# Gated attention stages of a hybrid transformer layer put back to back, with norms and routing inside them and expert work moved later

## What is computed

```
x = x + gated_attention(layernorm(x))   # "a": groups of 32 tokens, INNER 256
x = x + moe_ffn(layernorm(x))           # "f": 8 experts, top 2 of softmax(x @ Wr), capacity 160 a row
x = x + attention_16_heads(layernorm(x))# "c": softmax over 1024 x 1024 scores, 16 heads of 64
x = x + moe_ffn(layernorm(x))           # the same weights as the first FFN
```

## Time and profile before

| what | us |
|---|---|
| median of 3 runs | 1641.32 |
| the profiled execution | 1643.49 |
| its span, first to last instruction | 1641.5 |
| PE, DVE, ACT, POOL busy in the span | 1511.9, 1049.9, 881.9, 271.4 |
| start of the pairs (first L747) | 238.82 |

### The profile page before, as it was taken

One profiled execution on the slowest core, in us unless ns is written; L12 is line 12 of the kernel. 1 busy time (PEld: TensorE's weight loads), 2 busy tenths in 40 slices (PEclk: granted clock), 3 DMA queues, 4 the chain that ended last, 5 costly groups with the idle time before them and its releaser, 6 DMA issues.

```text
span 1641.5 us, 24653 instructions
## 1 busy us (share of the span) xinstructions
PE 1511.9 (92%) x9488; PEld 739.6 (45%) x9488; DVE 1049.9 (64%) x2187; ACT 881.9 (54%) x1697; POOL 271.4 (17%) x295
## 2 busy tenths in 40 slices
PE   6688989999999999999999999999999999999531
PEld 6587973333444333334443333344433334444231
DVE  6755837787555677865556888655568865556601
ACT  3334645555655555556555555665555555655221
POOL 3217443021000120200002103000021030000433
PEclk9799999999999999999999999999999999999766
DMA  8402121001000110110001101100021011000111
GB/s 236 153 22 68 40 71 39 14 25 35 14 14 14 39 30 14 33 33 7 14 14 42 45 21 30 30 14 14 3 56 36 14 32 27 14 14 1 44 43 55
DMA packets 45957, 60.05 MB, mean 37 GB/s; under 512 B 6915, under 2 KB 33952, under 8 KB 45712
## 3 DMA queue, kind: packets, MB, share of 16 engines
q1 hardware_dynamic: 36208, 39.57, 8.7%
q0 software_dynamic: 9632, 18.91, 4.0%
HBM read 23.83 MB, written 20.97 MB: 27 GB/s over the span
## 4 chain that ended last, share of the span: by engine, by line
PE 86%; DVE 3%; issue 3%; POOL 3%; DMA 2%; ACT 1%; POOLq 0%; DVEq 0%; ACTq 0%; SPq 0%
PE bank L801 30%; PE bank L811 27%; PE bank L747 8%; PE bank L762 4%; PE bank L752 4%; POOL xslots L499 3%; PE bank L910 2%; PE bank L905 2%; PE bank L322 2%; PE bank L311 1%; DMA slots_sb<-xslots 1%; PE bank L618 1%; PE bank L900 1%; POOL yg L510 1%; ACT hT L411 1%
## 5 line engine op out<-in xcount | busy, mean ns | idle before, releaser
L828 ACT ACTIVATE prob<-bank,nmx 128x1024 f32<-128x1024 f32 x512 | 565.9, 1110 | 513.6 <-DVE nmx L819 513.6
L819 DVE TENSOR_REDUCE nmx<-bank 128x1 f32<-128x1024 f32 x512 | 603.1, 1220 | 212.0 <-PE bank L801 211.7
L801 PE MATMUL bank<-q,k 64*128 64x512 f32 x1024 | 509.9, 616 | 2.5 <-ACT prob L828 1.7
L801 PE MATMUL bank<-q,ks 64*128 64x512 f32 x1024 | 506.5, 616 | 0.0
L811 PE MATMUL bank<-prob,vsc 128*64 128x512 f32 x2048 | 485.3, 595 | 0.0
L801 PEld LDWEIGHTS bank<-q,k 64*128 64x128 f32 x1024 | 170.6, 186 | 209.7 <-issue 127.7
L801 PEld LDWEIGHTS bank<-q,ks 64*128 64x128 f32 x1024 | 170.6, 186 | 122.3 <-issue 117.6
L811 PEld LDWEIGHTS bank<-prob,vsc 128*64 128x64 f32 x2048 | 139.8, 137 | 186.7 <-issue 184.2
L1214 POOL DMA_INDIRECT yg<-yslots,row_ring x80 | 80.5, 1006 | 811.2 <-PE bank L801 791.9
L835 DVE RECIPROCAL zinv<-zsum 128x2 f32<-128x2 f32 x256 | 42.4, 165 | 184.2 <-ACT prob L828 183.6
L747 PE MATMUL bank<-xT,wqkv_sb 128*64 128x512 f32 x512 | 137.4, 617 | 0.0
(11 more groups left out here) (209 smaller groups left out, 1395.4 us busy)
## 6 DMA issues: line engine op xcount, KB each, us to landing
ks<-k SPq DMA_DIRECT2D x64, 256.0 KB, 3.1
slots_sb<-xslots SPq DMA_DIRECT2D x8, 640.0 KB, 4.6
yslots<-slots_sb SPq DMA_DIRECT2D x8, 640.0 KB, 3.7
xslots<-xhat_r POOLq DMA_DIRECT2D x5, 512.0 KB, 7.1
yslots<-xhat_r POOLq DMA_DIRECT2D x5, 512.0 KB, 13.0
w_sb<-in_w SPq DMA_DIRECT2D x1, 2048.0 KB, 8.3
wqkv_sb<-in_wqkv SPq DMA_DIRECT2D x1, 2048.0 KB, 18.7
xslots<-xhat_r,row_s POOLq DMA_INDIRECT x128, 2.2
```

Of the source, the lines that this page charges most:

```text
L801: ins = nc.tensor.matmul(bank[:, SC[h][n], :], kk[r, cols(j)], qst[pi % 2][r, cols(n, HALF)], start=True, stop=True)
L819: nc.vector.tensor_reduce(nmx[:, 2 * s + h:2 * s + h + 1], bank[:, SC[h][0]:SC[h][0] + 2, :], mybir.AxisListType.XY, ALU.max, negate=True) ...
L828: nc.scalar.activation(prob[s][h][:].rearrange("p (n c) -> p n c", c=HALF), bank[:, SC[h][0]:SC[h][0] + 2, :], ACT.Exp, bias=nmx[:, 2 * s ...
```

## The change

Rows 0, 1 and 2 of the attention now run without experts between them; experts 0 follow stage 2, then stage 3, experts 1, experts 2 and the pairs. The pieces between the stages move into them:

- The norm of the next row, and from stage 1 on the norm of the row before for its FFN, are split: DVE makes mean, variance and rstd and a shift (`norm_stats_vector`), ACT writes the normed row (`xhat_scalar`, eight activations in place of DVE's L212), PE transposes it inside the stage, before L618. ACT waits, before it overwrites `xhat_r` in stages 2 and 3, for the scatter of the row before last (`f_sc`).
- Logits and the choice of experts of row r - 1 come at the end of stage r. The counts and slot numbers of row 0 come in the middle of stage 2 (PE waits for `f_idx` ahead of its last two token blocks of v); those of rows 1 and 2 in experts 0 and 1.
- The bias that DVE added (L219) is now added by POOL (`a_bias_gpsimd`), ahead of the scatters. PE waits for the residual of the stage before (`a_res`) ahead of v, and for all four v's ahead of the linear scores (v's banks are swapped).
- Answers go to a buffer of their own (`ans_sb`), so that a row's slots can be loaded while the answers of the one before are still stored. `xslots` and `yslots` are four tensors each; only `xslots` is zeroed, with 2.6 MB where 5.2 MB were written.
- Only row 0 is gathered in the head. Rows 1 and 2 are gathered and combined beside steps 0 to 33 of the pairs (`first_gathers`, `COMBINE_0`).
- In the tail DVE's statistics come ahead of a wait, and two small copies go (`wtok`, `row_g`).

The core of the diff:

```diff
+        def norm_stats_vector(v, step, c0, b, done):
+
+            stats_vector(v, step, c0, b, range(T))
+            aggr_vector(v, step, c0)
+            newton_vector(v, step, c0, NEWTON, True)
+            c = slice(c0, c0 + T)
+            nc.vector.scalar_tensor_tensor(out=shift[:, c], in0=meanvar[:, c, 0], scalar=-1.0, in1=rstd[:, c],
+                                           op0=ALU.mult, op1=ALU.mult).then_inc(done, 1)
+
+        def xhat_scalar(a, c0, b, xh, done):
+
+            for t in range(T):
+                c = c0 + t
+                ins = nc.scalar.activation(xh[:, t, :], row_of(b, t), ACT.Identity, bias=shift[:, c:c + 1], scale=rstd[:, c:c + 1])
+                if t % 4 == 3:
+                    ins.then_inc(done, 1)
+
...
-        V_BANK = [0, 1, 6, 7]
+        V_BANK = [6, 7, 0, 1]
...
+        def a_tensor(pe, r):
+            if r == B - 1:
+                pe.wait_ge(f_idx, 2)
...
+            if r > 0:
+                pe.wait_ge(a_res, 2 * r)
             for t in range(T):
                 if t == 4:
                     pe.wait_ge(a_xs, 2 * r + 2)
+                    if r == 2:
+                        positions(pe, 0)
+                if t == 6 and r == 2:
+                    pe.wait_ge(f_idx, 1)
                 x_hi, x_lo, o = xT_hi[:, cols(t)], xT_lo[:, cols(t)], bank[:, V_BANK[t // 2], cols(t % 2, INNER)]
                 nc.tensor.matmul(o, x_hi, wa_hi[:, WVA:], start=True, stop=False)
                 nc.tensor.matmul(o, x_hi, wa_lo[:, WVA:], start=False, stop=False)
...
-            pe.wait_ge(a_vbias, 4 * r + 2)
+            pe.wait_ge(a_vbias, 4 * r + 4)
...
-            if with_experts:
-                pe.wait_ge(a_state, 7 * (r + 1))
+                if e == 0 and r > 0:
+                    f_norm_tensor(pe, r - 1, FTR)
+            if r < B - 1:
                 pe.wait_ge(a_gated, 4 * r + 2)
-                slots_tensor(pe, r - 1, THIRD_A)
+                a_norm_tensor(pe, r + 1, ATR)
+            if r > 0:
+                logits_tensor(pe, r - 1, LG)
...
+            if r > 0:
+                a.wait_ge(lf_stat, r)
+                if r > 1:
+                    a.wait_ge(f_sc, 256 * (r - 1))
+                xhat_scalar(a, 0, r - 1, xhat_r, lf_xhat)
...
+            if r < B - 1:
+                a.wait_ge(la_stat, r + 1)
+                a.wait_ge(la_tr, 2 * r + 2)
+                xhat_scalar(a, T, r + 1, xhat, la_xhat)
+            if r > 0:
+                f_norm_scalar(a, r - 1, FTR)
+            if r < B - 1:
+                a_norm_scalar(a, r + 1, ATR)
+            if r > 0:
+                probs_scalar(a, r - 1)
+
+        def a_vector(v, step, r):
+            b = r
+            if r > 0:
+                norm_stats_vector(v, step, 0, r - 1, lf_stat)
...
+            if r == 2:
+                route_place_vector(v, step, 0, 0)
...
+            if r < B - 1:
+                if r == 0:
+                    v.wait_ge(load_x, 16)
+                norm_stats_vector(v, step, T, r + 1, la_stat)
...
+            if r > 0:
+                route_choose_vector(v, step, r - 1, LG)
+            if r < B - 1:
+                a_low_vector(v, r + 1)
+            v.wait_ge(a_bias, r + 1)
...
+        def a_bias_gpsimd(p, r):
+
+            xb = xres[:, r * T:(r + 1) * T, :]
+            hold(p, la_xhat, 2 * r + 2)
+            nc.gpsimd.tensor_tensor(xb, xb, bout_sb[:].unsqueeze(1).to_broadcast([P, T, P]), ALU.add).then_inc(a_bias, 1)
...
+        COMBINE = {2: (0, 0, 4), 3: (0, 4, 8), 5: (1, 0, 4), 6: (1, 4, 8)}
+        COMBINE_0 = {5: (1, 0, 0, 4), 6: (1, 0, 4, 8), 8: (1, 1, 0, 4), 9: (1, 1, 4, 8),
+                     30: (2, 0, 0, 4), 31: (2, 0, 4, 8), 32: (2, 1, 0, 4), 33: (2, 1, 4, 8)}
...
+        def first_gathers(p):
+
+            for m, g0 in ((1, 0), (2, 10)):
+                hold(p, f_comb, 2 * T * m)
+                hold(p, f_st, 16 * (m + 1))
+                for k in range(2):
+                    for t in range(T):
+                        if t % 2 == 0:
+                            paced(p, g0 + (k * T + t) // 2)
+                        gather_tile(p, m, k, t, f_ga)
...
+            for b in range(B):
+                nc.gpsimd.dma_start(xslots[b][0:S, :].rearrange("(t p) c -> p t c", p=P), xhat_r[:]).then_inc(zeroed, 16)
+                nc.gpsimd.dma_start(xslots[b][S:, :].rearrange("(t p) c -> p t c", p=P), xhat_r[:, 0:ST - T, :]).then_inc(zeroed, 16)
             p.wait_ge(zeroed, ZEROED)
-            for b in range(B):
-                if b > 1:
-                    gather(p, step, b - 1, b - 2)
-                if b < B - 1:
-                    scatter(p, b + 1)
+            for r in range(3):
+                a_bias_gpsimd(p, r)
+            scatter(p, 0, 0)
+            a_bias_gpsimd(p, 3)
+            scatter(p, 1, 1)
+            gather(p, 0, 0)
+            scatter(p, 2, 2)
...
+            for r in range(3):
+                a_scalar(a, r)
+                if r == 1:
+                    a.wait_ge(zeroed, ZEROED)
+            a.wait_ge(load_f, 112)
+            slots_scalar(a, 0)
+            experts_scalar(a, 0, lambda e: None)
+            a_scalar(a, 3)
+            slots_scalar(a, 1)
+            experts_scalar(a, 1, lambda e: None)
+            slots_scalar(a, 2)
+            experts_scalar(a, 2, lambda e: first_norm_scalar(a) if e == E else None)
...
+            a_low_vector(v, 0)
+            for r in range(3):
+                a_vector(v, step, r)
+            route_place_vector(v, step, 1, 1)
+            a_vector(v, step, 3)
+            route_place_vector(v, step, 2, 2)
+            combine_vector(v, step, 0, 0)
...
+            a_tensor(pe, 0)
+            pe.wait_ge(load_f, 112)
+            a_tensor(pe, 1)
+            a_tensor(pe, 2)
+            pe.wait_ge(la_xT, 8)
+            pe.wait_ge(f_sub, 2)
+            slots_tensor(pe, 0)
+            experts_tensor(pe, 0, lambda e: positions(pe, 1) if e == 1 else None, (a_res, 6))
+            a_tensor(pe, 3)
+            pe.wait_ge(f_sub, 3)
+            slots_tensor(pe, 1)
+            experts_tensor(pe, 1, lambda e: positions(pe, 2) if e == 1 else None, (a_res, 8))
+            slots_tensor(pe, 2)
+            experts_tensor(pe, 2, lambda e: first_norm_tensor(pe, 2) if e == E else None, (f_ys, 6))
```

More of the change, by code:

```diff
@@ L215, in bias_vector @@
-        def bias_vector(v, step, n, b, bias):
-            xb = xres[:, bass.ds(b * T, T), :]
-            v.wait_ge(ln_xhat, (n + 1) * T)
-            step.done(nc.vector.tensor_tensor(xb, xb, bias[:].unsqueeze(1).to_broadcast([P, T, P]), ALU.add))
-        def xT_scalar(a, n):
-            for h in range(2):
-                c = slice(h * HALF, (h + 1) * HALF)
-                a.wait_ge(ln_tr, 2 * n + h + 1)
-                nc.scalar.activation(xT[:, c], bank[:, LN_MAIN + h, :], ACT.Copy).then_inc(ln_xT, 1)
-                a.wait_ge(ln_xT, 2 * n + h + 1)
-                nc.scalar.activation(xT_hi[:, c], xT[:, c], ACT.Copy).then_inc(ln_hi, 1)
@@ L243, in ln_scalar, with row_of, stats_vector @@
-        def ln_scalar(a, n, dst, bk):
-            for h in range(2):
-                a.wait_ge(ln_tr, 2 * n + h + 1)
-                nc.scalar.activation(dst[:, h * HALF:(h + 1) * HALF], bank[:, bk + h, :], ACT.Copy).then_inc(ln_xT, 1)
         def cols(i, n=P):
             return slice(i * n, (i + 1) * n)
+        def row_of(b, t):
+            return xres[:, b * T + t, :]
+        def stats_vector(v, step, c0, b, tiles):
+            for t in tiles:
+                step.done(nc.vector.bn_stats(stats[:, c0 + t, :], row_of(b, t)))
@@ new lines, in xhat_scalar, with transposes @@
+        def xhat_scalar(a, c0, b, xh, done):
+            for t in range(T):
+                c = c0 + t
+                ins = nc.scalar.activation(xh[:, t, :], row_of(b, t), ACT.Identity, bias=shift[:, c:c + 1], scale=rstd[:, c:c + 1])
+                if t % 4 == 3:
+                    ins.then_inc(done, 1)
+        def transposes(pe, xh, half, bk):
+            for t in range(4):
+                ins = nc.tensor.transpose(bank[:, bk, cols(t)], xh[:, 4 * half + t, :], ident[:])
+            return ins
@@ new lines, in a_norm_tensor, with a_norm_scalar @@
+        def a_norm_tensor(pe, r, bk):
+            for h in range(2):
+                pe.wait_ge(la_xhat, 2 * r + h + 1)
+                transposes(pe, xhat, h, bk + h).then_inc(la_tr, 1)
+        def a_norm_scalar(a, r, bk):
+            for h in range(2):
+                c = cols(h, HALF)
+                a.wait_ge(la_tr, 2 * r + h + 1)
+                nc.scalar.activation(xT[:, c], bank[:, bk + h, :], ACT.Copy).then_inc(la_xT, 1)
+                a.wait_ge(la_xT, 2 * r + h + 1)
+                nc.scalar.activation(xT_hi[:, c], xT[:, c], ACT.Copy).then_inc(la_hi, 1)
@@ new lines, in a_low_vector, with f_norm_tensor, f_norm_scalar @@
+        def a_low_vector(v, r):
+            for h in range(2):
+                c = cols(h, HALF)
+                v.wait_ge(la_hi, 2 * r + h + 1)
```

(21 more changed lines are left out.)

473 lines of the change are left out of this document (172 added, 301 removed).

## The result

The changed kernel takes 1669.77 us (median of 4, 1668.21 to 1670.82), the kernel before, beside it, 1641.99 (4 runs, 1640.40 to 1643.72): ratio 1.0168, 95% interval 1.0151 to 1.0186. The profiled execution has a span of 1669.0 against 1641.5, so 27.5 of it can be read in the traces.

A forecast was written before the change was run, and what follows sets the result against it. The head was taken to go at the pace of a loop of route, scatter, load and experts; pairs 17.9 later plus 0.5 within them made 18.4, hence 1661.9 profiled and 1659.7 us forecast, 8 in 10 within 1650 to 1669.

The forecast's parts named there:

- row 1 starts at 45.3: End of stage 0: row 1's first projection on PE starts at 45.3 us, 20 us gained so far.
- full-clock unit: A stage's PE work at full clock: 11.5, 9.9 and 3.6 us, 25.0 in all, with the out-projection taking 3.84.
- Stage 1: Stage 1: 33.2 us of PE work with additions, out-projection done at 78.5, then PE stands 2.5 until 81.5.
- the wait in stage 2: ACT waits for row 0's scatter before overwriting `xhat_r`; PE stands 21.5 us, from 101.3 to 122.8.
- The wait before the last slots: In experts 2, PE stands 13.7 us for row 2's scatter and load; slots reach it at 232.9.
- the faster one: Rival: ACT finds row 0's scatter through and stage 2 runs on; pairs at 234.4, time 1637.4; chance 0.07.
- Late weights: Rival: zeroing isn't shortened, w2 lands at 51.8, PE stands 6.5 us at 45.3; time 1666; chance 0.06.
- Low clock for longer: Rival: after stands of 21 and 14 us, stage 2 stays at half clock through its sums, +5: 1665; chance 0.10.
- POOL's bias: Rival: through the shared port the bias blocks DVE's low part, 0 to 10 us; 1665 at 5 each; chance 0.06.
- cancelled the loss: Rival: gains elsewhere, DVE's stretches 10% shorter and the last wait halved, cancel the loss: 1641; chance 0.02.
- Pairs: Pairs: four more quarters of a combination on DVE add 0.5 us, ends 0 and 4.5.
- table-load drain: Exp loads ending stages 1 and 2: skill's 1380 ns drain would add 1.4 at the first; left out.

The follow-up runs named there:

- fifteenth run: Changed kernel with PE kept busy at the ends of stages 0 to 2, row 0 handed over by tiles, POOL's bias behind the low part: 1667.49 us, ratio 1.0154.
- fourteenth run: Changed kernel with row 0's normed rows handed to PE tile by tile, not by halves: 1669.79 us, ratio 1.0163.
- seventh run: Changed kernel with all four stages ahead of the experts and a second buffer for row 1's normed FFN rows: 1638.07 us, ratio 0.9970.
- thirteenth: Changed kernel with PE multiplying constants while it would stand at the ends of stages 0 to 2: 1668.88 us, ratio 1.0154.
- tenth: Changed kernel with ACT's scatter wait and `xhat_r` activations moved behind v's silus, keys and squares: 1694.9 us beside 1702.8 for the kernel before.
- seventeenth: Changed kernel with ACT's scatter wait and `xhat_r` activations moved behind v's silus, keys and squares: 1650.48 us, ratio 1.0051.
- third run: Changed kernel with PE multiplying constants while it would stand at the ends of stages 0 to 2: 1709.1 us beside 1712.3 for the kernel before.
- fourth run: Changed kernel with POOL's bias waiting for both low parts of the next row: 1710.1 us beside 1712.3 for the kernel before.
- first run: Changed kernel with a second buffer for row 1's normed FFN rows: 1695.2 us beside 1712.3 for the kernel before.

## Why the prediction came out low

The order of events was right, and so were direction and cause. The steps, in us on each clock: as forecast, in the changed kernel, and with the three sizes mended (fifteenth run):

```
                          forecast  changed  mended
row 1 starts                 45.3    49.89    46.02
row 2 starts                 81.5    86.83    81.37
slot numbers of row 0        93.9    98.27    94.44
key-value products 2        122.8   127.18   123.34
stage 2 done                143.5   149.62   145.93
experts 0 done              166.1   172.12   168.42
stage 3 done                197.1   205.29   199.46
slot numbers of row 2       205.3   213.47   207.64
slots of row 2 on PE        232.9   240.94   235.22
pairs start                 256.7   265.45   259.56
```

**The step that failed** is "row 1 starts at 45.3": the length of stage 0, 4.6 of the 8.8 us by which the pairs are later than forecast. Three terms were mis-sized, two by going on with full clock and the old hand-over.

(1) The key-value products start at 29.54, in the forecast's trace at 27.30. Row 0 is handed over by halves, an edit that I had not costed: the first projection starts at 15.15 instead of 14.40, which is 0.75. The rest is when the products quicken: they come 0.43 apart until 21.3 instead of 17.1. That moment varies in the same code: the kernel before, run again (sixth), starts these products at 28.82. Over all profiled executions they start at 28.2 to 29.5 by halves (fifteen, mean 28.9) and at 27.3 to 28.8 by tiles (five, mean 27.9). So the hand-over is worth about 1 us, and what the fourteenth run shows, 2.0, is in part luck.

(2) PE stands 2.6 us for the gates, which I had; the out-projection behind it then runs at a granted 0.50 and takes 5.76, which I had at 3.84. Kept busy, it took 3.74. The trace of before had the warning. I took its full-clock unit from stage 0, but behind PE's waits for slots the same 32 products took longer in stages 1 to 3:

```profile
95.88 5.37 PE L618 MATMUL bank<-wout_sb,gateT 128*128 128x128 f32 x32
...
154.70 4.99 PE L618 MATMUL bank<-wout_sb,gateT 128*128 128x128 f32 x32
...
213.98 4.39 PE L618 MATMUL bank<-wout_sb,gateT 128*128 128x128 f32 x32
```

(3) ACT's eight activations took 3.18, not 2.4; this lay within the bounds.

Part of the 4.6 is chance. In the eleven profiled executions that leave stage 0 as it is, row 1 starts between 46.9 (seventh run) and 49.9 (the profile above): never as early as forecast, and the profile above is the latest of them.

**Stage 1** came out right as a sum, 36.9 us against 36.2, by two errors that cancel: I had PE done with the out-projection at full clock and then standing for DVE's low part; in fact the out-projection took 6.46 and hid that wait. Kept busy (thirteenth) it took 3.82, PE stood 2.2 for the low part, and from row 1's start to row 0's numbers are 48.4 us in both. The path from row 2's start to the numbers (11.4 against 12.4) was near. So was **the wait in stage 2**: 28.9 us from numbers to key-value products, forecast 28.9; PE stood 21.05, forecast 21.5. The edit that takes it away gave 26.5 us, the one that frees what is queued behind it 19.3. The wait before the last slots was 13.0, forecast 13.7.

**The other half**: behind the key-value products stage 2 took 22.4 against 20.7 (its out-projection 5.30, again partly at the lower clock), stage 3 took 33.2 against 31.0 (its key-value products 4.95, behind a stand of 3.8, where stage 1's took 3.19), experts 2 24.5 against 23.8. In the fifteenth run stage 3 takes 31.0; of the 2.9 us left there at the pairs, 1.9 lie behind the key-value products of stage 2. Why the clock fell behind a stand of 0.46 and 0.82 in stage 2 is open; one product ahead of each didn't raise it (5.45), but in the tenth and seventeenth runs, where PE doesn't stand there, the out-projection took 3.82.

**Of the rivals**, the faster one needed that ACT not wait; it waited 28 us, so it fell, though with the wait gone the kernel comes out at 1644.6, not 1637. Late weights: w1 and w2 were issued at 25.6 and 26.2, no wait for them. Low clock for longer was the right kind of mechanism in the wrong place: I put it behind the long stands of 21 and 14 us; behind the first the key-value products took 4.92, less than the 5.3 of the sum, and what the sum lacked came behind stands of 1 to 4 us. POOL's bias took 2.36 each; it slows DVE's low part, off the path. Nothing cancelled the loss: the last wait was not halved. Pairs: +0.3, forecast 0.5. The Trainium skill's table-load drain (ScalarE: Activation LUTs, What ACT_TABLE_LOAD costs) wasn't seen: the exp load of stage 1 starts at 80.45, 0.01 after the activation ahead of it, takes 1.28, and the exp starts at 81.75; so it is at the silu load of the seventh run (84.69, silu at 85.99).

## What to carry to other kernels

Look for what is queued behind a wait on an in-order engine: the same wait cost 21 us of PE with the silus behind it and 10 with them ahead of it, and nothing with a second buffer. A transfer chain of 28 us wants a whole stage beside it each time; ask of a new order how many of them keep one. When a chain is placed at full clock, look at each stand of even 1 to 3 us and at the matmuls right behind it, and bound these by what they take at the lower clock (here 5.3 to 6.7 us for 3.8). And before a gain of 1 or 2 us is read from one trace of each kernel, see how far the same stretch moves in the same code: here by 3 us.

## What the runs showed of the hardware

The clock behind a short stand is not a fixed answer. After the same stand of 2.60 us at the end of stage 0 (2.59 in the changed kernel) the seventh run's windows show

```profile
43.00:47.00 4.00, 4.00 (x37) 4.00 (x38) 2.95 (x3) 2.10 (x4) 2.36 (x1) 1.00 0.58 232
```

and an out-projection of 3.74; the changed kernel's show 0.50, and it takes 5.76. The Trainium skill (TensorE: Matmul & The Clock Gate, Part 1) ties the clock to recent activity; the third run's raised clock agrees, the seventh shows that a trace of one execution doesn't settle it.

At the kernel's start the granted clock reads 1.00 while products take the longer time (0.63, next start 0.43 on; from 21.5 on 0.39 and 0.23):

```profile
16.00:20.00 4.00, 4.00 (x11) 3.01 (x11) 1.26 (x2) 3.29 (x5) 2.62 (x4) 1.00 1.03 262
```
```profile
20.40 0.63 PE L534 MATMUL bank<-xT_hi,wa_hi 128*128 128x512 f32 x1
...
21.52 0.40 PE L534 MATMUL bank<-xT_hi,wa_hi 128*128 128x512 f32 x1
```

On the disturbed occasions engines stand with "remote" as the releaser, that is for nothing that the trace shows on their own core; here ACT in the fourth run's experts 1, PE behind it:

```profile
256.05 0.39 ACT L386 ACTIVATE yT<-bank,b_sb 128x160 f32<-128x160 f32 x1 [8.62 <-remote]
```
```profile
261.71 4.01 PE L328 MATMUL bank<-hT,w_sb 128*128 128x160 f32 x16 [10.11 <-ACT hT L380]
```

The stands lay ahead of the pairs and behind them, hardly in them: in the first run PE is busy for 1295.7 us of the 1312 from 276 us on, where the changed kernel undisturbed has 1299.2. Two chips showed them, and both gave undisturbed times on another occasion, so it isn't the chip; what it is stays open.
